# A macaron block with two routed FFNs: unchecked row transfers, logits in column groups, a choice of experts in three parts, and eight row buffers

## The reference

```python
x = x + 0.5 * moe_ffn(layernorm(x))      # 8 experts, the two best per token, F = 176
x = x + attention(layernorm(x))          # 16 heads of 16, rotary embedding, causal
x = x + 0.5 * moe_ffn(layernorm(x))      # the same weights again

def moe_ffn(xn):
    logits = xn @ gate_w.T
    w, e = top_k(logits, 2);  w = softmax(w)
    return sum_k w[k] * (silu(xn @ w_gate[e[k]]) * (xn @ w_up[e[k]])) @ w_down[e[k]]
```

## Time and profile before

| | us |
|---|---|
| median of three runs (lowest, highest) | 1274.49 (1272.66, 1275.88) |
| the profiled execution | 1275.83 |
| its span in the trace | 1274.1 |
| busy PE, DVE, ACT, POOL | 1030.9, 857.1, 644.3, 602.0 |

### The profile page before, as it was taken

One profiled execution on the slowest core, in us unless ns is written; L12 is line 12 of the kernel. 1 busy time (PEld: TensorE's weight loads), 2 busy tenths in 40 slices (PEclk: granted clock), 3 DMA queues, 4 the chain that ended last, 5 costly groups with the idle time before them and its releaser, 6 DMA issues. The chain is left out here.

```text
span 1274.1 us, 23457 instructions
## 1 busy us (share of the span) xinstructions
PE 1030.9 (81%) x6726; PEld 636.6 (50%) x6726; DVE 857.1 (67%) x2599; ACT 644.3 (51%) x1318; POOL 602.0 (47%) x758
## 2 busy tenths in 40 slices
PE   1847998881878479999999999999987559988850
PEld 1326987771767323333333333333275239977750
DVE  5584444432999498989998998899267664444437
ACT  1503554442766406766666666666864305544520
POOL 1926777773998502222222222222204917777750
PEclk9957999995999759999999999999988859999975
DMA  6702222213465511111111111100004402222239
GB/s 220 245 0 73 96 98 98 99 72 101 128 191 171 163 66 46 63 59 60 57 58 56 57 51 59 59 35 2 1 2 127 142 9 95 91 94 97 97 105 343
DMA packets 84521, 117.46 MB, mean 92 GB/s; under 512 B 11806, under 2 KB 64812, under 8 KB 81328
## 3 DMA queue, kind: packets, MB, share of 16 engines
q1 hardware_dynamic: 63424, 75.04, 18.3%
q0 software_dynamic: 13632, 33.59, 7.8%
q10 hardware_dynamic: 7344, 7.34, 1.6%
HBM read 75.48 MB, written 43.78 MB: 94 GB/s over the span
## 5 line engine op out<-in xcount | busy, mean ns | idle before, releaser
L1306 ACT ACTIVATE a_probs<-a_ps_s 128x1024 f32<-128x1024 f32 (+3 forms) x384 | 294.3, 813 | 173.2 <-PE a_ps_s L1338 171.9
L1221 POOL TENSOR_SCALAR_AFFINE_SELECT a_probs<-a_probs 128x256 f32<-128x256 f32 x256 | 102.5, 406 | 369.8 <-ACT a_probs L1306 367.0
L1239 DVE CUSTOM_DVE_ANT_0 a_unused<-a_ps_m,const_sb 128x128 bf16<-128x128 f32 (+3 forms) x512 | 234.2, 485 | 26.7 <-PE a_ps_m L1323 16.7
L1323 PE MATMUL a_ps_m<-st_k,st_q 96*128 96x512 bf16 (+3 forms) x768 | 219.7, 344 | 23.8 <-PEq L157 16.5
L358 POOL DMA_INDIRECT v_sb<-xn_dram,f_token_i x142 | 145.4, 1024 | 100.7 <-issue 68.8
L1241 DVE TENSOR_REDUCE a_max_a<-a_ps_m 128x1 f32<-128x512 f32 x256 | 175.8, 687 | 14.3 <-PE a_ps_m L1323 13.9
L1338 PE MATMUL a_ps_s<-st_q,st_k 98*128 98x512 bf16 (+3 forms) x768 | 180.8, 329 | 1.5 <-ACT a_probs L1306 1.4
L495 DVE TENSOR_TENSOR f_h<-f_ps_gu,f_sg 128x176 f32<-128x176 f32 x142 | 48.5, 342 | 176.7 <-ACT f_sg L563 175.6
L1323 PEld LDWEIGHTS a_ps_m<-st_k,st_q 96*128 96x128 bf16 x768 | 67.9, 98 | 196.1 <-DVE a_max_a L1241 55.7
L1351 PE MATMUL a_ps_ctx<-a_probs,a_v_st 128*32 128x512 f32 (+3 forms) x1536 | 163.6, 498 | 1.3 <-POOL a_probs L1221 0.6
L363 POOL DMA_INDIRECT y_dram<-v_sb,f_pair_i x142 | 143.6, 1011 | 43.4 <-issue 40.1
(11 more groups left out here) (180 smaller groups left out, 2035.9 us busy)
## 6 DMA issues: line engine op xcount, KB each, us to landing
xn_dram<-v_sb SPq DMA_DIRECT2D x64, 128.0 KB, 4.3
p_yb<-y_dram SPq DMA_DIRECT2D x32, 256.0 KB, 2.8
v_sb<-y_dram SPq DMA_DIRECT2D x32, 256.0 KB, 5.8
st_q<-qk_dram SPq DMA_DIRECT2D x16, 384.0 KB
st_k<-qk_dram SPq DMA_DIRECT2D x16, 384.0 KB
qk_dram<-st_rT_hi SPq DMA_DIRECT2D x16, 256.0 KB, 2.8
qk_dram<-st_rT_mid SPq DMA_DIRECT2D x16, 256.0 KB, 3.1
qk_dram<-st_rT_lo SPq DMA_DIRECT2D x16, 256.0 KB, 4.0
```

Source lines behind the costliest of these rows:

```text
L1221: pool.affine_select(out=tri, in_=tri, compare_op=ALU.is_ge, fill=zero, base=0, pattern=[[0, 2], [1, P]], channel_multiplier=-1).then_inc( ...
L1239: dve.tensor_tensor_reduce(unused[:, bank, 0:nk], ps, cst("mask")[:, HALF - nk:HALF], 1.0, NEG, ALU.add, ALU.max, at).then_inc(taken, 1)
L1306: act.activation(probs[:, s % 4, :, 0:nq], ps_s[s % 2][:, :, 0:nq], ACT.Exp, scale=float(HD) ** -0.5).then_inc(exp_done, 1)
L1323: pe.matmul(ps_m[bank][:, 0:nk], q_st[b][0:MAX_ROW, h, P * i:P * i + P], k_st[b][0:MAX_ROW, h, k0:k0 + nk], start=True, stop=True).then_in ...
```

## The change

It has five parts.

- The row transfers of the FFN run without `bounds_check`. An empty slot's pair number now points to an own row behind the 8192 rows of `y_dram` (the constant `past`), which grows by 71 x 128 rows, and its token number is masked into the range of `xn_dram`. The memset of `xg` goes.
- The logits are computed in four column groups of 32: the gate's weights are padded with zeros to 32 columns, and tile u of four writes partitions 32u to 32u + 31 of one 128 x 128 result, in eight matmuls of 128 tokens. DVE copies 128 columns instead of 512, and one full transpose, one step earlier, replaces the four small ones. The logits lie in two PSUM banks, now one tensor.
- `choose_two` takes a range of tiles: tiles 0 to 15 before the turned tiles 20 to 23 are copied, 16 to 23 before tiles 28 to 31, and 24 to 31 at the end. `hot_ready` counts to three.
- The gap is computed ahead of the lots of one-hot matrices, and the mixing weights behind them.
- The projection has eight buffers of rows (`YB`), which lie in the last q and k buffers of the ring, now with all 128 partitions. Six loads stand ahead of the steps, and each step loads the tile 15 ahead, with the wait for the tile eight before it. `stacks.fill` moves into attention's SP program, behind a load and ahead of `send_max`, and PE's wait for it to the first unit of the second pass.

```diff
@@ -73,6 +73,7 @@
     put("tile256", np.tile(TOPK * P * np.arange(NT), TOPK))
+    put("past", TOPK * T + 1 + p[:, None] + P * np.arange(SLOT_TILES)[None, :])
     put("low", TOPK * p[:, None] + np.arange(TOPK)[None, :] + 1)
@@ -192,7 +193,7 @@
         xnT = carve(P, 2, KD, 4 * P)
-        lgT = carve(E, 2, 4 * P)
+        lgT = carve(P, 2, P)
         after_lgT = carved[0]
@@ -257,11 +258,13 @@
         ps_hT = [bank[0:FH, :, :] for bank in ps_hT_bank]
-        ps_y = [pb(f"ps_y{i}", [P, D]) for i in range(2)]
+        ps_y_banks = pb("ps_y", [P, 2, 2 * D])
+        ps_y = [ps_y_banks[:, i, 0:D] for i in range(2)]
         ps_turn = [bank[:, :, :] for bank in ps_xT + ps_hT_bank]
-        ps_lgT = [bank[0:E, :] for bank in ps_gu]
-        ps_lg = ps_y[0][:, 0:NT * E].rearrange("p (t e) -> p t e", e=E)
+        ps_lgT = [bank[:, 0:P] for bank in ps_gu]
+        ps_logits = ps_y_banks[:, :, :].rearrange("p y (t e) -> p (y t) e", e=GP)
+        ps_lg = ps_logits[:, :, 0:E]
         ps_before = ps_gu[1][:, 0:E * NT].rearrange("p (e t) -> p e t", e=E)
@@ -348,20 +351,14 @@
-            pool.memset(xg, 0.0).then_inc(pool_init, 1)
-            pool.wait_ge(pool_init, 1)
             pool.wait_ge(slots_ready, 1)
-            last_token, last_pair = pool.to_reg(T - 1), pool.to_reg(TOPK * T - 1)
             def gather(slot, token):
-                pool.indirect_dma_start(xg[:, slot, :], None, xn_dram, bass.IndirectOffsetOnAxis(ap=token, axis=0),
-                                        bounds_check=last_token, oob_is_err=False).then_inc(gathered[slot], 16)
+                pool.indirect_dma_start(xg[:, slot, :], None, xn_dram, bass.IndirectOffsetOnAxis(ap=token, axis=0)).then_inc(gathered[slot], 16)
...
                 pool.wait_ge(y_out, j + 1)
-                pool.indirect_dma_start(y_dram, bass.IndirectOffsetOnAxis(ap=pair, axis=0), y_sb[:, slot, :], None,
-                                        bounds_check=last_pair, oob_is_err=False).then_inc(scattered[slot], 16)
+                pool.indirect_dma_start(y_dram, bass.IndirectOffsetOnAxis(ap=pair, axis=0), y_sb[:, slot, :], None).then_inc(scattered[slot], 16)
@@ -394,40 +391,41 @@
+            def choose_two(t0, t1):
+                of, by_tile = slice(t0, t1), [P, t1 - t0, E]
+                below = cst("below").unsqueeze(1).to_broadcast(by_tile)
+                def over_experts(x):
+                    return x.unsqueeze(2).to_broadcast(by_tile)
+                def choose(c, logits):
+                    own.then_wait(dve.tensor_reduce(best[:, c, of], logits, AX.X, ALU.max))
+                    own.then_wait(dve.tensor_tensor(is_best[:, of, :], logits, over_experts(best[:, c, of]), ALU.is_equal))
+                    own.then_wait(dve.tensor_tensor(is_best[:, of, :], is_best[:, of, :], below, ALU.mult))
+                    own.then_wait(dve.tensor_reduce(chosen[:, c, of], is_best[:, of, :], AX.X, ALU.min))
+                    own.then_wait(dve.tensor_tensor(hot[:, c, :, of].rearrange("p e t -> p t e"), below, over_experts(chosen[:, c, of]), ALU.is_equal))
+                dve.wait_ge(lg_ready, t1 // 4)
+                choose(0, ps_lg[:, of, :])
+                own.then_wait(dve.scalar_tensor_tensor(others[:, of, :], hot[:, 0, :, of].rearrange("p e t -> p t e"), NEG, ps_lg[:, of, :], ALU.mult, ALU.add))
+                choose(1, others[:, of, :])
+                dve.tensor_tensor(hot_sum[:].rearrange("p (e t) -> p e t", e=E)[:, :, of], hot[:, 0, :, of], hot[:, 1, :, of], ALU.add).then_inc(hot_ready, 1)
+            own.inc(dve.tensor_copy(before_bf[:], cst("before")))
+            own.then_wait(dve.memset(ones_bf[:], 1.0))
             for i in range(NT // 4 + 1):
+                if i == 5:
+                    choose_two(0, 16)
+                if i == 7:
+                    choose_two(16, 24)
                 for u in range(4):
...
                         copy_logits(i - 1)
-            own.inc(dve.tensor_copy(before_bf[:], cst("before")))
-            own.then_wait(dve.memset(ones_bf[:], 1.0))
...
-            dve.tensor_tensor(gap[:], best[:, 1, :], best[:, 0, :], ALU.subtract).then_inc(gap_ready, 1)
-            dve.wait_ge(egap_ready, 1)
-            own.then_wait(dve.tensor_scalar(den[:], egap[:], 1.0, None, ALU.add))
-            own.then_wait(dve.reciprocal(gap[:], den[:]))
-            own.inc(dve.tensor_scalar(w_mix[:, 0, :], gap[:], 0.5, None, ALU.mult))
-            own.inc(dve.scalar_tensor_tensor(w_mix[:, 1, :], egap[:], 0.5, gap[:], ALU.mult, ALU.mult))
+            choose_two(24, NT)
@@ -452,6 +450,7 @@
+            dve.tensor_tensor(gap[:], best[:, 1, :], best[:, 0, :], ALU.subtract).then_inc(gap_ready, 1)
             dve.wait_ge(count_ready, 2)
@@ -463,12 +462,18 @@
                                   ALU.is_equal).then_inc(one_hot_ready, 1)
+            dve.wait_ge(egap_ready, 1)
+            own.then_wait(dve.tensor_scalar(den[:], egap[:], 1.0, None, ALU.add))
+            own.then_wait(dve.reciprocal(gap[:], den[:]))
+            own.inc(dve.tensor_scalar(w_mix[:, 0, :], gap[:], 0.5, None, ALU.mult))
+            own.inc(dve.scalar_tensor_tensor(w_mix[:, 1, :], egap[:], 0.5, gap[:], ALU.mult, ALU.mult))
             dve.wait_ge(owner_ready, 1)
             in_tile = ps_owner[:, SLOT_TILES:2 * SLOT_TILES]
-            own.then_wait(dve.tensor_scalar(empty[:], in_tile, 0.0, EMPTY, ALU.is_equal, ALU.mult))
+            own.then_wait(dve.scalar_tensor_tensor(empty[:], in_tile, 0.0, cst("past"), ALU.is_equal, ALU.mult))
             own.then_wait(dve.scalar_tensor_tensor(low[:], in_tile, -1.0, empty[:], ALU.add, ALU.add))
             own.then_wait(dve.tensor_tensor(pair_i[:], ps_owner[:, 0:SLOT_TILES], low[:], ALU.add))
-            dve.tensor_scalar(token_i[:], pair_i[:], 1, None, ALU.logical_shift_right).then_inc(slots_ready, 1)
+            dve.tensor_scalar(token_i[:], pair_i[:], 1, T - 1, ALU.logical_shift_right, ALU.bitwise_and).then_inc(slots_ready, 1)
@@ -602,25 +607,25 @@
                 for k in range(KD):
-                    mm = pe.matmul(ps_lgT[i % 2], gate_sb[:, k, :], xnT[:, i % 2, k, :], start=(k == 0), stop=(k == KD - 1))
+                    for u in range(4):
+                        mm = pe.matmul(ps_lgT[i % 2][GP * u:GP * (u + 1), :], gate_sb[:, k, :], xnT[:, i % 2, k, u * P:(u + 1) * P],
+                                       start=(k == 0), stop=(k == KD - 1), skip_group_check=True)
                 mm.then_inc(logits_done, 1)
...
                 pe.wait_ge(lgT_ready, i + 1)
-                for u in range(4):
-                    mm = pe.transpose(ps_lg[:, 4 * i + u, :], lgT[:, i % 2, u * P:(u + 1) * P], ident[0:E, 0:E])
-                mm.then_inc(lg_ready, 1)
-            for i in range(NT // 4 + 2):
+                pe.transpose(ps_logits[:, 4 * i:4 * i + 4, :].rearrange("p t e -> p (t e)"), lgT[:, i % 2, :], ident).then_inc(lg_ready, 1)
+            for i in range(NT // 4 + 1):
                 for u in range(4):
...
                         turn(4 * i + u)
-                    if u == 1 and 0 < i <= NT // 4:
+                    if u == 1 and i > 0:
                         logits(i - 1)
-                if i >= 2:
-                    turn_back(i - 2)
-            pe.wait_ge(hot_ready, 1)
+                if i >= 1:
+                    turn_back(i - 1)
+            pe.wait_ge(hot_ready, 3)
             pe.matmul(ps_before.rearrange("p e t -> p (e t)"), before_bf[:], hot_sum[:], start=True, stop=True)
@@ -714,7 +719,7 @@
-YB = 4
+YB = 8
 RTS = 3
@@ -787,8 +792,11 @@
         self.qk_dram = qk_dram
-        self.q = [sb(f"q{i}", [ROWS, HG, S]) for i in range(RING)]
-        self.k = [sb(f"k{i}", [ROWS, HG, S]) for i in range(RING)]
+        whole_q, whole_k = [[sb(f"{qk}{i}", [P, HG, S]) for i in range(RING)] for qk in "qk"]
+        self.q, self.k = [[whole[0:ROWS, :, :] for whole in stack] for stack in (whole_q, whole_k)]
+        self.before_last = [whole[RING - 1][:, :, :].rearrange("p h s -> p (h s)").bitcast(F32).rearrange("p (y c d) -> p y c d", c=TOPK, d=D)
+                            for whole in (whole_q, whole_k)]
         self.one = ctx.enter_context(nc.sbuf_tensor("st_one", [HG * TB, P], BF16))
@@ -881,6 +888,10 @@
+        def yb(t):
+            return stacks.before_last[t % YB // 4][:, t % 4, :, :]
         def beside(rT, u):
@@ -889,7 +900,7 @@
                 wait(sp, mixed, t - YB + 1)
-                sp.dma_start(yb[:, t % YB, :, :].rearrange("p c d -> p (c d)"),
+                sp.dma_start(yb(t).rearrange("p c d -> p (c d)"),
                              y_dram[t * P * TOPK:(t + 1) * P * TOPK, :].rearrange("(p c) d -> p (c d)", c=TOPK)).then_inc(y_in[t % YB], 16)
@@ -906,16 +917,15 @@
             def step(t, u):
-                if is_tile(t + AHEAD + 3):
-                    load_y(t + AHEAD + 3)
+                if is_tile(t + AHEAD + 1 + YB - 2):
+                    load_y(t + AHEAD + 1 + YB - 2)
                 if t >= 5 and t % 2 == 1:
...
-            for t in range(2):
```

(19 more changed lines are left out.)

26 lines of the change are left out of this document (5 added, 21 removed).

## The result

The changed kernel takes 1254.53 us (median of four runs, 1253.2 to 1256.25) where the kernel before takes 1274.3: a ratio of 0.9846, with an interval of 0.9828 to 0.9864, or 20 us less. The forecast was 1237, 39 us less; the range held.

A forecast was written before the change was run, and what follows sets the result against it. POOL was taken to bound both expert stages, after a serial routing chain, and DVE and POOL together the projection. Routing 11, transfers 17 and projection 11 sum to 39 us: 1275.8 - 39 = 1237, range 1191 to 1260.

The forecast's parts named there:

- rival B: FFN row transfers: the check costs POOL nothing, so dropping it gains nothing; 1254 us, chance 0.24.
- Unchecked transfers: FFN gathers and scatters without the check: 0.06 us saved on each of 142 x 2 transfers, 17 us.
- The bound from below: FFN gathers: the last, skipping every row, takes 1.03 us like the 1.025 mean, so the check may be worth nothing.
- Rival C: Expert stages: the check costs 0.19 us or more per transfer, so PE becomes the bound; 1200 us, chance 0.22.
- The choice in three parts: Routing, DVE: parts of 5.8, 4.9 and 4.9 us, the third ending at 67.4, 3.1 us earlier than before.
- rival D: Routing: every part pays the full wait for POOL's instructions; gain 1.2 us per FFN, not 5.7; 1246 us, chance 0.10.
- the column logits: Routing: PE's period of four tiles falls by 1.4 us; DVE's logits copy shrinks from 0.68 to 0.29 us.
- Its better bound: Routing: without waits for POOL, 1.5 us less per part, the gain is 8 to 10 us per FFN.
- Mixing weights later: Routing: the scan starts at 71.2 instead of 74.02 us; 2.8 less 0.2 for the gap, 2.6 us per FFN.
- Eight row buffers: Projection: start 6.5 us earlier and the later stall of 4.5 us gone; sum 11 us.
- the bound of 5.4: Attention: the moved fills cost at most 5.4 us if the first pass does not hide them.
- Rest: One memset in setup and two-operation forms of existing instructions: below 0.3 us.

## Why the prediction was right, and where it was not

**The range and the sign held; the time came out near rival B for another reason.** B's 1254 was the case in which the check is free and the routing gains 11. Measured: the check is worth 11.4 us in the two expert stages and the routing 3.0. Two misses together gave B's number, so that the time lies at 1254 is luck and speaks for nothing in B.

**Unchecked transfers.** Right in kind, mis-sized: 0.06 us per transfer forecast, 0.040 measured (the mean of 55 and 24 ns), 11 us instead of 17. The bound from below, taken from a gather without rows at 1.03 us, was not informative: a check that is paid whether or not a row moves looks the same. Behind B the prediction set the rule of the Trainium skill, DMA: Bandwidth & Descriptors, section "Anatomy of one DMA", that many descriptors go out before their cost shows. That rule is about descriptors and names no check; carried over to one, as in B, it made the forecast 11 us too long, because the check took 4% of a transfer's 1.02 us on POOL. Rows that are now moved instead of skipped are hidden, as said. Rival C, PE as the bound, did not come near.

**The choice in three parts** is the step that failed. The prediction let the first part start at 44.9, gave the parts 5.8, 4.9 and 4.9 us, and had the third end at 67.4. Measured: start 46.26, parts 6.6, 6.0 and 5.5, and 4.7 and 3.6 us between them where 3.9 and 3.0 were forecast, end 72.60. Held time is 2.2, 2.6 and 2.1 us per part, not half of 3, over the 4.3 and 3.4 undisturbed. The last logits with their copy and transpose, 1.3 us by the estimate, took 2.1 from 65.06 to 67.12, with PE at half its clock after its pause. So rival D named the mechanism: it left 1.2 us per FFN for the whole routing, and 1.7 and 1.3 were measured, nearer to it than to 5.7. (D's 1246 us missed all the same, since the transfers, the start and setup brought less than it took over from the forecast.) Behind that small gain stand larger terms: the column logits bring 2.3 us, the mixing weights 2.1, and the three parts take 3.0 to 3.7 back against one choice. The prediction compared the parts with the kernel before only, never with one choice behind the column logits, and so counted as their gain what the logits bring alone. Its better bound, 8 to 10 us per FFN without held time, falls too: with POOL idle the three parts end no earlier than one choice. The Trainium skill, SBUF — State Buffer, section "SBUF: two separate sides", with its lock between VectorE's instructions with two SBUF inputs and GpSimd, agrees with the traces: of the twelve instructions of a choice only those with two SBUF inputs are held, for up to 2.87 us where they need 0.29, and none when POOL is idle. Outside the choice, instructions with one SBUF operand were held as well (1.44 us instead of 0.17 for the one in the mixing weights).

**Mixing weights later.** 2.6 us per FFN forecast, 2.0 and 2.3 measured alone, and hidden where the prediction put them. The scan won the forecast time; some of it was lost behind it to a held instruction.

**Eight row buffers.** The stall went to the full 4.5 us. The start gave 4.3 and not 6.5: the sum let POOL mix a tile every 0.74 us, but the second tile's row landed late (ACT's second weighing starts at 292.96, 1.46 us idle), and DVE, with a second mixing and the moments for each tile, reached the aggregation of the first four only at 298.20. It is DVE and the loads that pace the start. The fills in attention cost 0.15 us of the bound of 5.4.

**Rest.** Below 0.3 us was forecast; setup became about 1 us longer, and the cause stays open.

**The chances.** "Faster" at 0.92 was right. D at 0.10 was too low: the row that spoke for it (1.77 us where 0.42 is needed) stood in the prediction, and it gave each part half of the held time where the trace shows at least two thirds of it in each.

## What to carry to other kernels

Cutting a serial step into parts that overlap pays only if the engine has idle time there and its neighbours leave it alone. Count the parts' fixed and held costs, and what queues behind them on the same engine, and compare with the same work in one piece behind the other edits, not with the kernel before. Before moving work away from a contended port, ask which engine's instructions hold it: here the gain came from giving a third of POOL's weight splitting to ACT, while delaying POOL's work only moved the wait. And count what a pause does to the engine that waits: here PE came back at half its clock.

## What was not expected of the hardware

- The check of an indirect transfer costs POOL 55 ns per gather and 24 ns per scatter of 128 rows, whether rows are skipped or not. Why the two differ was not tried; the last scatters, with no gather between them, went only from 0.98 to 0.97 us.
- Held time goes both ways: POOL's subtraction of 704 columns took 2.55 us beside DVE's lots and 1.68 alone.
- POOL can go first twice. Beside casts and subtractions in turn, a product of two SBUF operands in a choice took at most 1.89 us and ended behind one POOL instruction; beside subtractions alone it took 2.18 and 2.87 and ended behind the second. That the pause between POOL's instructions decides this is argued from these traces and was not tried by itself.
